# Attention's normalized x turned by VectorE in 32x32 blocks by way of DRAM, in place of TensorE transposes; layer-norm statistics one tile earlier

## The reference, cut to what matters

```python
def step(carry, qkv_t):                      # linear attention, one token
    kv_s, k_s = carry
    q_t, k_t, v_t = qkv_t
    kv_s = kv_s + jnp.einsum('bhe,bhf->bhef', k_t, v_t)
    k_s = k_s + k_t
    num = jnp.einsum('bhe,bhef->bhf', q_t, kv_s)
    den = jnp.einsum('bhe,bhe->bh', q_t, k_s)[..., None] + EPS_DEN
    return ((kv_s, k_s), num / den)
...
h = _layernorm(x, axis=-1) * (1 + ca) + sa
x = x + ga * _L0_attn_ref(h, W_qkv, b_qkv, W_out, b_out)   # q, k, v = split(h @ W_qkv + b_qkv)
h = _layernorm(x, axis=-1) * (1 + cb) + sb
x = x + gb * _L0_ffn_ref(h, w_gate, w_up, w_down)
```

## Time and profile before

| | us |
|---|---|
| median of 3 runs (range) | 1997.45 (1996.22 to 1999.36) |
| the profiled execution, its own time | 1998.45 |
| its span, first to last instruction | 1996.7 |
| busy in the span: PE / DVE / ACT / POOL | 1960.6 / 1443.1 / 905.7 / 877.4 |
| attention groups 2 to 13 | about 59.05 each |
| mean granted TensorE clock | 0.998 of full speed |

### The profile page before, as it was taken

How to read it: one execution, slowest core, us unless ns; L and a number is a source line. 1 busy time by engine, 2 the same in 40 slices (tenths; PEclk the granted TensorE clock), 3 DMA queues, 4 the chain that set the end, 5 groups by cost and what they waited for, 6 DMA issues and landing times. The chain is left out here.

```text
span 1996.7 us, 43856 instructions
## 1 busy us (share of the span) xinstructions
PE 1960.6 (98%) x16008; PEld 1591.9 (80%) x16008; DVE 1443.1 (72%) x2386; ACT 905.7 (45%) x1542; POOL 877.4 (44%) x718
## 2 busy tenths in 40 slices
PE   7999999999999999999899999999999999999999
PEld 4788888888888888887678888788888888888887
DVE  7977888878788878787865857658576585765744
ACT  5443444344444434443344535445354453544533
POOL 2533544444544444453334443444434444344444
PEclk9999999999999999999999999999999999999999
DMA  7223333444434434432575654656546565465553
GB/s 268 69 91 102 115 123 119 135 130 133 135 100 133 128 125 135 127 110 90 179 263 176 207 187 145 214 170 209 186 144 215 171 210 186 144 214 174 169 168 106
DMA packets 202521, 309.81 MB, mean 155 GB/s; under 512 B 16145, under 2 KB 72977, under 8 KB 202386
## 3 DMA queue, kind: packets, MB, share of 16 engines
q1 hardware_dynamic: 201858, 306.78, 48.1%
q10 hardware_dynamic: 528, 1.05, 0.1%
HBM read 225.19 MB, written 82.58 MB: 154 GB/s over the span
## 5 line engine op out<-in xcount | busy, mean ns | idle before, releaser
L1497 POOL TENSOR_TENSOR h_lo<-y_rows,h_hi 128x512 fp32r<-128x512 f32 x192 | 246.5, 1301 | 367.6 <-ACT h_hi L1595 367.6
L461 POOL TENSOR_TENSOR x_res<-y,x_res 128x512 f32<-128x512 f32 x64 | 86.6, 1353 | 294.0 <-DVE y L872 283.5
L851 DVE TENSOR_TENSOR probs<-sc,causal 128x512 f32<-128x512 f32 x256 | 158.5, 681 | 3.8 <-PE sc L1156 2.6
L612 ACT ACTIVATE z_exp<-pj,qk_neg 128x512 f32<-128x512 f32 x128 | 87.7, 686 | 161.5 <-PE pj L1137 158.0
L1137 PE MATMUL pj<-xt_hi,w_hi 128*128 128x512 f32 x512 | 145.9, 406 | 5.7 <-DVE a_t L861 4.7
L1925 PE MATMUL sc<-wd,h_hi 128*128 128x512 f32 x384 | 150.7, 392 | 0.0
L1925 PE MATMUL sc<-wd,h_lo 128*128 128x512 f32 x384 | 149.6, 389 | 0.0
L450 POOL TENSOR_TENSOR a_lo<-a_t,a_hi 128x512 fp32r<-128x512 f32 x60 | 82.2, 1370 | 144.8 <-ACT a_hi L626 144.8
L1137 PE MATMUL pj<-xt_lo,w_hi 128*128 128x512 f32 x512 | 138.1, 391 | 1.8 <-DVE xt_lo L789 1.8
L1137 PE MATMUL pj<-xt_hi,w_lo 128*128 128x512 f32 x512 | 138.1, 392 | 0.0
L1710 DVE TENSOR_TENSOR r_den<-pj,k_tok 128x512 f32<-128x512 f32 x96 | 66.3, 691 | 97.9 <-ACT k_tok L1578 52.2
(11 more groups left out here) (248 smaller groups left out, 5390.4 us busy)
## 6 DMA issues: line engine op xcount, KB each, us to landing
w_hi<-parts SPq DMA_DIRECT2D x48, 1024.0 KB, 5.4
w_lo<-parts SPq DMA_DIRECT2D x48, 1024.0 KB, 5.4
x_mid<-x_res SPq DMA_DIRECT2D x96, 256.0 KB, 2.8
x_res<-in_L_attn_x SPq DMA_DIRECT2D x64, 256.0 KB, 2.8
k_dram<-k_block SPq DMA_DIRECT2D x252, 64.0 KB
xg<-in_L_attn_x SPq DMA_DIRECT2D x15, 1024.0 KB, 7.4
x_res<-x_mid SPq DMA_DIRECT2D x60, 256.0 KB, 3.9
full<-x_mid SPq DMA_DIRECT2D x60, 256.0 KB, 3.7
```

Source lines behind the costliest of these rows:

```text
L461: pool.tensor_tensor(out=x_res[:, slot, :], in0=y[:, :], in1=x_res[:, slot, :], op=ALU.add).then_inc(y_ready, 1)
L612: act.activation(z_exp[:, n % 2, :], pj[:, n % 2, :], ACT.Relu, bias=qk_neg[:, 1 - kind, c:c + 1], scale=-scale).then_inc(below_ready, 1)
L851: dve.tensor_tensor(out=probs[:, h, :].rearrange("p (c i) -> p c i", c=C), in0=sc[:, h, :].rearrange("p (c i) -> p c i", c=C), in1=causal[ ...
L1497: pool.tensor_tensor(out=h_lo[b], in0=h[i], in1=h_hi[b].bitcast(F32), op=ALU.subtract).then_inc(h_lo_ready, 1)
```

## The change

For groups 2 to 15, `x_turn` on TensorE goes. In its place, ScalarE's queue writes the normalized `xg` (1 MB) to a DRAM tensor `x_norm` (`save_x`), waits until it has landed, and issues four reads of 256 KB (`load_blocks`) that bring it back into `xg` in such a way that a 32x32 block transpose of the whole buffer, one DVE instruction on 128x2048 (`turn_x`), gives x with features on partitions. The reads move runs of 128 numbers (512 bytes) into 32 partitions each. `xt_full` then reads SBUF instead of PSUM. The feature order inside the buffer changes, so the rows of `W_qkv` and the modulation rows are reordered on the host, and groups 0 and 1, still turned by TensorE, get a reordered copy of x. To make room for the round trip, `norm_stats` and `norm_var` move up into tile 0 and `norm_x` to the head of tile 1; on SP `load_group` moves ahead of `load_units`, and it now waits for `xt_full` instead of the transposes; on POOL `rstd_of` moves up.

In the diff, the first piece is SP's list, then ScalarE's two new functions, VectorE's `turn_x`, three pieces of VectorE's list (tiles 0, 1 and 2), and TensorE's `front`; `rest` loses its `x_turn` under the same condition.

```diff
 def group(g, parity):
-    if not isinstance(g, int):
-        load_units(g, parity)
     if not isinstance(g, int) or g + 2 < NG:
         load_group(g + 2)
+        if not isinstance(g, int):
+            load_units(g, parity)
...
+def save_x(g):
+    wait(act, xn_ready, g + 1)
+    act.dma_start(x_norm.rearrange("(t p) d -> p t d", p=P), xg[:, :, :]).then_inc(x_saved, 16)
+
+def load_blocks(g):
+    wait(act, x_saved, g * 16 + (-16))
+    for h in range(HPC):
+        act.dma_start(xg[h * E:(h + 1) * E, :, :].rearrange("p t (b x) -> p (t b) x", x=P),
+                     x_norm[:, h * P:(h + 1) * P].rearrange("(b i) x -> i b x", i=E)).then_inc(x_blocks_in, 16)
...
+def turn_x(g):
+    wait(dve, x_blocks_in, g * (16 * HPC) + (-16 * HPC))
+    blocks = xg[:, :, :].rearrange("p t d -> p (t d)")
+    dve.transpose(blocks, blocks).then_inc(xt_ps, C)
...
     mask(g * GT)
     if not first:
         v_rows(g, parity, 3)
+        norm_stats(g + 2)
...
     feature(n, other, 0)
+    if not first:
+        norm_var(g + 2)
...
-    norm_stats(g + 2, range(0 if first else 3, GT))
-    norm_var(g + 2)
+        norm_x(g + 2)
...
     feature(n, other, 6)
-    xt_low(g + 2, parity, 0)
+    if turned and not first:
+        turn_x(g + 2)
     feature(n, other, 7)
     gate_last(g, 2)
...
-    if t >= 2:
+    if t >= 2 and isinstance(g, int) and g + 2 == NG:
         wait(pe, probs_ready, (g * GT + t) * HPC + 4)
         x_turn(g + 2, 2 * t - 4, x_bank)
```

More of the change, by code:

```diff
@@ L304, in load_group @@
         def load_group(g):
-            wait(sp, xt_ps, C * g)
-            sp.dma_start(xg[:, :, :], x_groups[g, :, :, :] if isinstance(g, int) else
+            if isinstance(g, int) and g < 3:
+                wait(sp, xt_ps, C * g)
+            else:
+                wait(sp, xf_ready, C * g)
+            sp.dma_start(xg[:, :, :], x_first_groups[g, :, :, :] if isinstance(g, int) and g < 2 else
+                         x_groups[g, :, :, :] if isinstance(g, int) else
                          x_groups[bass.ds(g, 1), :, :, :].rearrange("a p t d -> (a p) t d")).then_inc(x_in, 16)
@@ L533, in group @@
             last_bias(g, 0)
+            if two_ahead and not (isinstance(g, int) and g == 0):
+                rstd_of(g + 2)
             if last:
@@ L544, in group @@
             last_bias(g, 1)
-            if two_ahead or last:
+            if last or isinstance(g, int) and g == 0:
                 rstd_of(g + 2)
@@ L684, in ahead_of_last @@
             looped = not isinstance(g, int)
+            g_last_turn = not looped and g + 2 == NG
+            at_start = not looped and g == 0
             exp_relu(n, 0)
@@ L692, in ahead_of_last @@
             exp_relu(n, 3)
+            if not g_last_turn and not at_start:
+                save_x(g + 2)
             exp_relu(n, 4)
@@ L700, in ahead_of_last @@
             exp_relu(n, 5)
+            if not g_last_turn:
+                if at_start:
+                    save_x(g + 2)
+                load_blocks(g + 2)
             exp_relu(n, 6)
-            xt_full(g + 2, 0, x_bank)
-            xt_high(g + 2, parity, 0)
+            if g_last_turn:
+                xt_full(g + 2, 0, x_bank)
             exp_relu(n, 7)
[L705 to L708, removed]
+            if g_last_turn:
+                xt_full(g + 2, 1, x_bank)
+            elif not at_start:
+                xt_full(g + 2, 0, x_bank)
+                xt_high(g + 2, parity, 0)
+                if looped:
+                    act.wait_ge(down_out, g * 16 + (-16))
+                xt_full(g + 2, 1, x_bank)
+                xt_high(g + 2, parity, 1)
             state_out(g * GT + 2)
@@ L712, in ahead_of_last @@
                 unit_to_float(g, parity, 1)
+            if at_start:
+                for c in range(2):
+                    xt_full(g + 2, c, x_bank)
+                    xt_high(g + 2, parity, c)
             xt_full(g + 2, 2, x_bank)
@@ L985, in ahead_of_last @@
             gate_last(g, 0)
-            if not first:
-                norm_stats(g + 2, range(3))
             divide(g * GT, g, parity, 0)
@@ L993, in ahead_of_last @@
             mask(g * GT + 1)
-            norm_stats(g + 2, range(0 if first else 3, GT))
-            norm_var(g + 2)
+            if first:
+                norm_stats(g + 2)
+                norm_var(g + 2)
+            else:
+                norm_x(g + 2)
             feature(n, other, 2)
@@ L1002, in ahead_of_last @@
             feature(n, other, 4)
-            norm_x(g + 2)
+            if first:
+                norm_x(g + 2)
             divide(g * GT + 1, g, parity, 1)
@@ L1016, in ahead_of_last @@
             den_of(n, 2)
-            xt_low(g + 2, parity, 1)
             if looped:
                 word_size(g, 2, r_den[other][:, 3, :], (unit_in[1], g * 16 + (-16)))
+            if not first:
+                xt_low(g + 2, parity, 0)
             mask(g * GT + 3)
             v_rows(n, other, 0)
+            if first:
+                turn_x(g + 2)
+                xt_low(g + 2, parity, 0)
             spread(g * GT + 3, g, parity, 3)
             k_blocks(n, other, 0)
+            xt_low(g + 2, parity, 1)
             den_of(n, 3)
@@ L1147, in scores @@
                 pe.wait_ge(wide_ready, 1)
-            if not isinstance(g, int) or g + 2 <= NG:
+            if isinstance(g, int) and g == 0:
+                pe.wait_ge(xf_ready, 2 * C)
+            elif isinstance(g, int) and g + 2 == NG:
                 wait(pe, xf_ready, (g + 2) * C + (0, 0, 0, 2)[t])
-            else:
+            elif isinstance(g, int) and g + 2 > NG:
                 wait(pe, xf_ready, (NG + 1) * C + (0, 0, 0, 2)[t])
@@ L1268, in rest @@
                 out_project(tile - 1)
-            if t >= 2 and ahead:
+            if t >= 2 and isinstance(g, int) and g + 2 == NG:
                 x_turn(g + 2, 2 * t - 3, x_bank)
@@ L1324, in feed_forward @@
 def feed_forward(sem, later, ident, mod_col, half_neg, norm, gb_dram, parts, att, shared, x_mid, out):
-    stats, mean_var, var_eps, rstd = norm[1:5]
+    stats, mean_var, var_eps, rstd, passed = norm[1:5] + norm[-1:]
     xg, xf, h_hi, h_lo, (blocks, filled), b_hi, b_lo, full, wd, total, saved, gate, h, y, x_res, gb_row, xs, sums, dn = shared
@@ L2021 @@
 _TURNED = ("L0_c",)
+REGROUPED = np.arange(D).reshape(HPC, C, E).transpose(1, 0, 2).reshape(D)
 def word_blocks(w_gate, w_up, w_down):
```

44 lines of the change are left out of this document (30 added, 14 removed).

## The result

The changed kernel takes 2094.82 us in the median (2090.11 to 2116.11, four runs; a fifth on record, 2104.38, lies inside), against 1997.39 for the kernel before beside it: a ratio of 1.0513, with a 95% interval of 1.0449 to 1.0577. It is slower by 5%, where 2012 us were forecast, and outside the range of 1980 to 2040.

The account below looks back on a forecast made before the run. The prediction took TensorE, busy 98% of the span, as the bound. From the profiled 1998.45 us: -26.0 - 3.7 + 21.3 + 19.5 + 3.6 = 2013.2; the median being 1.0 lower, 2012 us, range 1980 to 2040.

Parts of the forecast that it names:

- What is removed: TensorE's x_turn calls, 1.86 us a group, -26.0 us in 14 groups; the wait for divide, -3.7 us.
- Tile 0: Statistics ahead of gate_last wait for x (issued 1.9 us after scores start, S): TensorE waits 1.7 us a loop group, together +21.3.
- Tile 1: norm_x at the head and save_x's issue on ScalarE cost nothing; the write lands some 5 us later.
- Tile 2: Reads and block transpose ahead of gate_last: reads hidden, TensorE waits 1.5 us in groups 1 to 13, +19.5 us.
- The clock: TensorE's clock might fall at waits of 3.8 us, for 1.7 us each; not at 1.7 us; nothing in the sum.
- Group 0: ScalarE stands behind unit 5 until the write of x has landed, making numerators late: +3.6 us once.
- The round trip is hidden: Rival, chance 0.28: x lands early and both TensorE waits shrink to 0.3 us or less, 1976 us.
- The reads are late: Rival, chance 0.08: tile 2's reads land 7.4 us after the last issue, another 2.8 us in 13 groups, 2048 us.
- VectorE and POOL exclude each other: Rival, chance 0.08: norm_x in tile 1 meets POOL's work, 3.9 us, net 2 us more in 12 groups, 2036 us.

Follow-up runs that it names:

- run 10: Changed kernel reordered as in run 6, then divide(1) ahead of feature 4, reads behind unit 6, one normalization ahead of gate_last(1), group 14's flag earlier: 1975.45 us, ratio 0.9884.
- run 1: Changed kernel with the four statistics put back behind gate_last(0) and the aggregate behind divide: 2106.26 us, ratio 1.0546.
- run 5: Changed kernel with the statistics behind gate_last(0) and the weights (load_units) ahead of the load of x on SP: 2075.61 us, ratio 1.0394.
- run 4: Changed kernel without the DRAM write and the four reads, x turned only within blocks (attention not the reference's): 2049.71 us, ratio 1.0261.
- run 7: Kernel before the change, with three useless statistics instructions ahead of gate_last(0) to delay VectorE: 2017.15 us, ratio 1.0099.
- run 8: Kernel before the change, with five useless statistics instructions ahead of gate_last(0) to delay VectorE: 2067.25 us, ratio 1.035.
- run 6: run 5 plus norm_x before gate_last(1), write behind state_out(1), turn behind divide(2) and word_size, first xt_low in tile 3, ScalarE's xt_full later: 1994.95 us, ratio 0.9985.

## Why the prediction was wrong

The sign, both places and what TensorE waits for there were right; the sum was 103 us short of the profiled execution. What failed is the size of both waits, and a cost that the sum had at nothing, the clock. By the prediction's own steps:

- **What is removed** was right, and a little more: 2.0 us a group in place of 1.86, by TensorE's busy time in run 10.
- **Tile 0** failed by a size, the landing of x. It was taken to be issued at S + 1.9 and to land 5.0 us later; issues were at S + 2.2 in the mean, and the page of after shows 6.3. Below it stand the write and the reads, then the first and the fourth read of group 6 alone:

```profile
xg<-in_L_attn_x SPq DMA_DIRECT2D x14, 1024.0 KB, 6.3
x_norm<-xg ACTq DMA_DIRECT2D x14, 1024.0 KB, 4.4
xg<-x_norm ACTq DMA_DIRECT2D x56, 256.0 KB, 6.1
xg<-x_norm ACTq DMA_DIRECT2D x1, 256.0 KB, 4.4
xg<-x_norm ACTq DMA_DIRECT2D x1, 256.0 KB, 7.4
```

  VectorE idled 4.0 us in place of 2.0, and TensorE 3.55 in place of 1.7: the excess of the one is the excess of the other. 5.0 was a slope through loads of other stages; 6.3 lies inside the bounds of 4.5 and 7.4. The step also left a second wait unpriced, the weights that are now behind x on SP; run 1 against run 5 shows it: as soon as the statistics no longer hide it, it holds `gate_last` itself.
- **Tile 1** was right: no wait ahead of the scores of tile 2. The 4.4 us of the write agree with "some 5 us".
- **Tile 2** failed in one sentence, "I take them as hidden, by one microsecond". The reads go out from S + 5.0 to 6.5, earlier than thought, but in the mean of the loop the four land 4.5, 6.0, 6.8 and 7.6 us after their issues, not 2.4. The last is in at S + 14.1, where the step had 9.8 or 11.0, and VectorE, ready at S + 11.8 (11.98 in the step), waits 2.3 us for it. The rest of the step nearly held: the block transpose takes 2.31 us (2.4). Without the trip the wait is 1.10 us in run 4; the step without the 0.84 us of the four issues would give 0.7.
- **The clock** was the step that failed outright. "Stalls of 1.7 us are shorter than that gap" was true of stalls of 1.7 (run 7 shows 1.5 us to be free of it), but the bounds of both waits reached 3.8 and 4.0, and there the prediction wrote "they might do it, for 1.7 us each" and put nothing into the sum. It costs 4.6 us a group, 56 us in the loop, more than half of the miss. Runs 7 and 8 show it apart from everything else in the change.
- **Group 0** was forecast at +3.6, less the 1.86 of its transposes; its length is 61.23 us, against 55.5 before, so +5.7, and 4 short.

In us, from the forecast: 12 x (3.55 - 1.7) = 22, 12 x (3.55 - 1.5) = 25, 56 for the clock, 4 in group 0, less 2 for the transposes: 2013.2 + 105 = 2118, where the profiled execution took 2116.11.

**The rivals.** *The round trip is hidden* was priced at 1976, and run 10 takes 1975.45: what that rival described exists, in another order of the same work. That the numbers are so close is in part chance, since run 10 also gains 2 us in group 14, which is outside the rival. *The reads are late* came true: it had the last read 7.4 us after its issue, and that took 7.6 in the mean. The rival's wait ahead of tile 3 is 1.5 + 2.8 = 4.3 us (the bound of the step, for the same landing, says 4.0), and 3.55 was measured, as the reads were issued earlier. Its 2048 still falls short by the landing of x and the clock. *VectorE and POOL exclude each other* did not come true at the size that it needed: the mean of `norm_x`'s instructions, before and after, over the whole execution, is

```profile
L775 DVE TENSOR_SCALAR xg<-xg,mean_var,rstd 128x512 f32<-128x512 f32 x72 | 38.2, 592 | 0.0
```

```profile
L818 DVE TENSOR_SCALAR xg<-xg,mean_var,rstd 128x512 f32<-128x512 f32 x72 | 43.8, 667 | 0.0
```

which is 5.6 us in all, 0.4 in each of the 14 changed groups, where that rival needed 3.9.

What stays open in part: why x lands 6.3 us after issue and not 5.0. Groups 0 and 1 load x with no weights behind it, and the loop with them; the changed kernel's landings in the two stretches are

```profile
xg<-in_L_attn_x SPq DMA_DIRECT2D x2, 1024.0 KB, 5.7
xg<-in_L_attn_x SPq DMA_DIRECT2D x12, 1024.0 KB, 6.3
```

So 5.0 was some 0.7 too low even with nothing behind (the same two loads of the kernel before take 5.5), and another 0.6 goes with the loop. That the weights are the cause of these 0.6 is not shown, from two loads; the round trip is not, as run 4 has 6.3 in its loop without it.

## What to carry to other kernels

Where TensorE is the bound, price a wait of three to five microseconds at 1.6 to 2 times its length: the clock that falls is paid in the work behind it (85 us of waits and 56 of clock in the changed loop, 2.9 and 2.9 a group in run 8). From two to three it may be paid or not. Work taken off TensorE comes back only when the list of the engine that takes it over is ordered by what the next product waits for: `gate_last` first, and the new transfers' waits behind everything that is due earlier. When a transfer is moved ahead of another on one queue, or its wait into a list of work, look at who waits for what stands behind it, on each queue.

## What the runs showed of the hardware

**Reads into 32 partitions.** The same megabyte that is written from 128 partitions in 4.4 us comes back in four reads of 256 KB. The last lands 9.1 us after the first issue, in the mean of the changed kernel's loop, and the landings are 1.8, 1.5 and 1.3 us apart. The Trainium skill (SBUF — State Buffer, section "Can I just issue two DMAs to hit both halves?") says that transfers to different partition ranges follow one another rather than add up; landings that come one behind another, at nearly equal steps, agree. An estimate by that page's rate for 32 partitions, 189 GB/s (section "Door 1: The DMA port swizzle"), would be 1.4 us for 256 KB and 5.5 us for 1 MB; the steps are near the first.

**VectorE and POOL take turns in a scan.** In run 6, one VectorE scan meets POOL's work and another does not. VectorE's rows, then POOL's:

```profile
442.57 2.20 DVE L848 TENSOR_TENSOR_SCAN k_sum<-kt,k_past 128x512 f32<-128x512 f32 x1
462.26 1.28 DVE L848 TENSOR_TENSOR_SCAN k_sum<-kt,k_past 128x512 f32<-128x512 f32 x1
```

```profile
441.94 1.74 POOL L453 TENSOR_TENSOR prod<-k_sum,qt 128x512 f32<-128x512 f32 x1
443.65 2.21 POOL L463 TENSOR_TENSOR x_res<-x_res,gabo_row 128x512 f32<-128x512 f32 x1
```

The scan is 0.92 us longer among the two, and POOL's second instruction 0.9 us longer than the 1.30 us that it takes elsewhere. POOL's first ends at 443.68, the scan at 444.77 and POOL's second at 445.86: each ends 1.09 us after the one before. Over the whole of run 6, the 34 scans that meet no work of POOL take 1.22 to 1.29 us, and the 30 that meet some 2.18 in the median. The Trainium skill (SBUF — State Buffer, section "SBUF: two separate sides") calls the shared port of the two an exclusive lock, and these rows agree.
